# State-space steps of a small macaron network: two Vector instructions a step in place of four

## The reference, cut to what matters

```python
delta = jax.nn.softplus(jnp.einsum('blr,er->ble', dt, W_dt) + b_dt)
A = -jnp.exp(A_log)
dA = jnp.exp(delta[..., None] * A)
dBx = delta[..., None] * Bm[:, :, None, :] * xc[..., None]
def step(h, inp):
    dA_t, dBx_t = inp
    h = dA_t * h + dBx_t
    return (h, h)
y = jnp.einsum('bles,bls->ble', hs, Cm) + xc * Dp
```

## Time and profile before

| what | us |
|---|---|
| median of 3 runs | 843.04 |
| lowest, highest of them | 842.71, 849.75 |
| span of the profiled execution | 845.8 |
| VectorE busy in the span | 561.1 |
| TensorE busy in the span | 754.4 |

### The profile page before, as it was taken

The page is one execution under the profiler, slowest core; times in us unless marked ns, Lnnn a source line. Parts: engine busy times, 40 slices in busy tenths (PEclk is TensorE's granted clock), DMA queues, the critical chain, the costliest instruction groups (busy, mean ns, idle before and its releaser), DMA issues.

```text
span 845.8 us, 10714 instructions
## 1 busy us (share of the span) xinstructions
PE 754.4 (89%) x3807; PEld 522.9 (62%) x3823; DVE 561.1 (66%) x983; ACT 407.3 (48%) x600; POOL 254.9 (30%) x193
## 2 busy tenths in 40 slices
PE   4899979995789799999998999998789999788997
PEld 3587555652335366667876777775447776435775
DVE  4444699999969999975345547347854655953543
ACT  3354797666446876741232343351385432174221
POOL 0000059985436787960896000001000000000000
PEclk9899999999997999999998998999899999999999
DMA  8300022222101222216101000034000142000000
GB/s 287 109 2 1 2 63 76 73 74 66 50 27 44 66 71 70 76 50 189 43 1 21 1 1 1 13 76 111 28 2 1 52 108 66 3 27 1 1 0 26
DMA packets 30591, 41.75 MB, mean 49 GB/s; under 512 B 3753, under 2 KB 19955, under 8 KB 30515
## 3 DMA queue, kind: packets, MB, share of 16 engines
q1 hardware_dynamic: 29290, 40.91, 16.6%
q10 hardware_dynamic: 1252, 0.19, 0.2%
HBM read 36.73 MB, written 4.26 MB: 48 GB/s over the span
## 4 chain that ended last, share of the span: by engine, by line
PE 64%; DVE 14%; issue 8%; ACT 6%; DMA 5%; SPq 2%; POOL 1%; DVEq 0%; POOLq 0%; ACTq 0%
PE PS L501 34%; PE PS L868 7%; PE PS L601 3%; DVE PS L1997 3%; PE PS L1071 2%; PE PS L1054 2%; PE PS L832 2%; PE PS L646 2%; DVE shared L2005 1%; ACT shared L1580 1%; PE PS L751 1%; DMA scratch_k<-shared 1%; PE PS L852 1%; PE PS L459 1%; PE PS L936 1%
## 5 line engine op out<-in xcount | busy, mean ns | idle before, releaser
L2316 POOL TENSOR_TENSOR shared<-shared,route 128x1024 f32<-128x1024 f32 x64 | 151.4, 2370 | 78.5 <-DVE shared L2005 78.4
L501 PE MATMUL PS<-xnT,weights_r 128*128 128x256 f32 (+1 forms) x732 | 155.2, 359 | 0.5 <-issue 0.3
L501 PE MATMUL PS<-xnT,work_r 128*128 128x512 f32 (+1 forms) x596 | 153.0, 406 | 0.0
L2005 DVE TENSOR_TENSOR_SCAN shared<-shared,PS 128x512 f32<-128x512 f32 x128 | 148.8, 1204 | 0.0
L501 PEld LDWEIGHTS PS<-xnT,weights_r 128*128 128x128 f32 x732 | 114.1, 189 | 34.1 <-issue 20.6
L501 PEld LDWEIGHTS PS<-xnT,work_r 128*128 128x128 f32 (+1 forms) x596 | 112.5, 194 | 25.5 <-issue 1.3
L868 PE MATMUL PS<-shared,cf 128*128 128x512 f32 x256 | 123.3, 605 | 0.0
L1761 DVE TENSOR_TENSOR gated<-gated,PS 128x512 f32<-128x512 f32 (+1 forms) x52 | 35.7, 686 | 106.1 <-ACT gated L1239 106.1
L1239 ACT ACTIVATE gated<-PS 128x512 f32<-128x512 f32 (+1 forms) x52 | 31.1, 598 | 139.7 <-PE PS L501 132.0
L1522 ACT ACTIVATE shared<-shared,cols 128x512 f32<-128x512 f32 x128 | 83.6, 712 | 22.6 <-DVE shared L2005 18.8
L501 PE MATMUL PS<-weights_r,work_r 128*128 128x256 f32 (+1 forms) x624 | 89.5, 294 | 2.0 <-DVE work_r L1768 1.8
(11 more groups left out here) (232 smaller groups left out, 1083.2 us busy)
## 6 DMA issues: line engine op xcount, KB each, us to landing
route<-scratch_c SPq DMA_DIRECT2D x64, 256.0 KB, 3.2
shared<-in_L_ffn_W_dram SPq DMA_DIRECT2D x3, 1024.0 KB, 8.7
scratch_k<-shared SPq DMA_DIRECT2D x12, 128.0 KB
scratch_q<-shared SPq DMA_DIRECT2D x12, 128.0 KB
shared<-scratch_k SPq DMA_DIRECT2D x8, 192.0 KB
shared<-scratch_q SPq DMA_DIRECT2D x8, 192.0 KB
mamba_w<-in_L_ffn_w_dram SPq DMA_DIRECT2D x2, 704.0 KB, 5.3
beside<-in_L_ffn_w_dram SPq DMA_DIRECT2D x2, 704.0 KB, 7.7
```

Source lines behind the costliest of these rows:

```text
L501: last = nc.tensor.matmul(o, lhs[l], rhs[r], start=(start and i == 0), stop=(stop and i == 2))
L2005: v.tensor_tensor_scan(hst[:, (t % 2 * 2 + j) * T:(t % 2 * 2 + j + 1) * T], decay[t % D_SLOTS][:, j * T:(j + 1) * T], products[:, j * T:(j ...
L2316: nc.gpsimd.tensor_tensor(hc[:, u * 2 * T:(u + 1) * 2 * T].rearrange("p (c t) -> p c t", c=2), hst[:, (t % 2) * 2 * T:(t % 2 + 1) * 2 * T] ...
```

## The change

Per step VectorE issues one product with B of 1024 columns (B is read twice, by a stride of zero over the chunks) and one scan of 1024 columns. The scan runs through from the first chunk to the second. So that no state is carried across, the decay of the first token of each chunk is zero: all such columns of the ring are set to zero once, by VectorE ahead of sequence 0, and ScalarE's exponentials write only columns 1 to 511 of each chunk. The product of a step waits for the whole scan of the step before, the scan for the whole product. The semaphore counts are kept (each instruction now adds 2).

```diff
-                        nc.scalar.activation(decay[t % D_SLOTS][:, j * T:(j + 1) * T], delta_of[b][c], ACT.Exp,
+                        nc.scalar.activation(decay[t % D_SLOTS][:, j * T + 1:(j + 1) * T], delta_of[b][c][:, 1:T], ACT.Exp,
                                              scale=c_A[:, n + c * DS:n + c * DS + 1]).then_inc(s["dA"], 1)
...
+                    v.memset(decays.rearrange("p (s t) -> p s t", t=T)[:, :, 0:1], 0.0)
...
                 def times_b(t):
                     half = t // DS
                     dve.wait_ge(s["B"], base + t + 1)
-                    for j in range(2):
-                        c = 2 * half + j
-                        dve.wait_ge(s["scan"], HEAD + 2 * (base + t - 1) + j + 1)
-                        if t % DS == 0:
-                            dve.wait_ge(s[("dx", "dx_p")[half]], b * 2 + j + 1)
-                        v.tensor_tensor(products[:, j * T:(j + 1) * T], dx[:, c * T:(c + 1) * T], bank(B_BANK),
-                                        ALU.mult).then_inc(s["mul"], 1)
+                    dve.wait_ge(s["scan"], HEAD + 2 * (base + t))
+                    if t % DS == 0:
+                        dve.wait_ge(s[("dx", "dx_p")[half]], b * 2 + 2)
+                    v.tensor_tensor(products.rearrange("p (c t) -> p c t", c=2),
+                                    dx[:, 2 * half * T:(2 * half + 2) * T].rearrange("p (c t) -> p c t", c=2),
+                                    bank(B_BANK).unsqueeze(1).broadcast_to([P, 2, T]), ALU.mult).then_inc(s["mul"], 2)
 
                 def scan(t):
                     dve.wait_ge(s["hc"], HEAD + base + t - 1)
-                    for j in range(2):
-                        dve.wait_ge(s["dA"], 2 * (base + t) + j + 1)
-                        dve.wait_ge(s["mul"], HEAD + 2 * (base + t) + j + 1)
-                        v.tensor_tensor_scan(hst[:, (t % 2 * 2 + j) * T:(t % 2 * 2 + j + 1) * T],
-                                             decay[t % D_SLOTS][:, j * T:(j + 1) * T], products[:, j * T:(j + 1) * T],
-                                             0.0, ALU.mult, ALU.add).then_inc(s["scan"], 1)
+                    dve.wait_ge(s["dA"], 2 * (base + t) + 2)
+                    dve.wait_ge(s["mul"], HEAD + 2 * (base + t) + 2)
+                    v.tensor_tensor_scan(hst[:, t % 2 * 2 * T:(t % 2 + 1) * 2 * T], decay[t % D_SLOTS], products,
+                                         0.0, ALU.mult, ALU.add).then_inc(s["scan"], 2)
```

## The result

The changed kernel took 864.11 us (median of four runs, 860.7 to 864.64), the kernel before 844.96 us beside it (842.71 to 849.75). The two medians lie 19.15 us apart. The ratio worked out over the fast runs of both is 1.0196, with a 95% interval of 1.0149 to 1.0242: about 16.6 us, or 2%, slower. That the kernel is slower is clear of the noise; whether by a little less or a little more than 2% is not. A second set of runs gave 1.020 (1.014 to 1.026). The forecast was 12.4 us of loss and 855.4 us, so the direction and the kind of loss were right and the size a quarter too small. The range of 847 to 862 us was stated on a kernel before of 843.0 us: 864.11 lies 2 us above it, while 843.0 x 1.0196 = 859.6 lies inside. The profiled execution has a span of 862.9 us, 17.1 more than the 845.8 of before, and took 864.64 us in itself, 1.7 more than its span.

The account below looks back on a forecast made before the run. VectorE, full in the state-space steps, was taken as the bound; +6.5 us in sequence 0, +5.85 in sequence 1 and 0.1 for the memset made 12.4 us, so 843.0 + 12.4 = 855.4 us, range 847 to 862.

Parts of the forecast that it names:

- The bound: State-space steps: VectorE is full there and only there, and practically never waits for other engines.
- plain step: A step with no other VectorE work in between: 1.22 + 0.12 + 2.26 + 0.12 = 3.72 us for 3.42, +0.30.
- The pauses: In front of each merged product and scan on VectorE: 0.12 us each, in place of an overlap of 0.08.
- the row with the separate wait: Attention copy L2065, two waits in front, starts 0.13 us behind its neighbour; taken as the guide for 0.12.
- the row of the chain: Softplus chain: an instruction waiting for its neighbour by one semaphore starts after 0.04 us; taken as the lower bound.
- rival A: Each dependence between neighbours costs only 0.035 us: plain step 3.55 us, +3.3 us in all, 846.4 us; chance 0.14.
- the 47 steps that the sum counts: Steps 0 to 29 without other VectorE work behind: 22 in sequence 0, 25 in sequence 1, +0.30 us each.
- Steps with other work behind the scan: Eight steps in sequence 0, five in sequence 1, where the following work still overlaps: +0.10 us each.
- What came back: Shrinking VectorE waits: sequence 0, 0.46 (sums with D), 0.40 (taps); sequence 1, 0.37 (steps 3, 4), 1.06 (sums), 0.67 (end).
- Between the sequences: From step 30's product in sequence 0 the path is TensorE's, so only steps 0 to 29 count.
- Rival C: TensorE, idler in the steps, falls to 1.2 GHz in some three more stretches: +4 us, 859.4 us; chance 0.13.
- Rival B: Waits are free and fewer instructions win: a step of 3.32 us, 0.10 less, 839.5 us; chance 0.05.

Follow-up runs that it names:

- changed_again: The changed kernel as it is, run again beside the other experiments: 863.65 us against 846.73 for the kernel before, ratio 1.020.
- products_in_sbuf: The changed kernel with its products written to SBUF in place of PSUM banks 2 and 3: 934.32 us beside 847.41 for the kernel before, one run.
- zero_columns: The kernel before with only the memset of the first columns and the exponentials of 511 columns: 846.54 us beside 846.73, one run.
- count_one: The changed kernel with semaphore counts of 1 in place of 2, waits in their old order: 864.45 us beside 847.41 for the kernel before, one run.

## Why the prediction was right, and where it was short

**The bound** was read right: VectorE is full in the steps, and what a plain step gains in length comes out in the end. From the first product to the end of step 30's product in sequence 0, and from the first product to the opened banks in sequence 1, the kernel took 8.5 and 7.6 us longer, 16.1 in all, where 6.5 and 5.85 were forecast. **The pauses** were put at 0.12 each and measured 0.13. Taking the row with the separate wait over the row of the chain decided the forecast: had the chain's 0.04 been right, the loss would have been rival A's 3.3 us. The run with the neighbour's wait first has just that pause, and lost 7.6 us; so rival A's kernel exists, but it is not this one, and my sum for it was 4 us short too.

That the 0.12 came out so close is partly luck, for the earlier trace rows do not show a wait for a neighbour. The code in front of the copy L2065 (L2064 and the line before) waits for a product of TensorE and for a result of ScalarE that was long there, and the product ended at the same time as VectorE's instruction ahead:

```profile
615.50 0.86 PE L1071 MATMUL PS<-shared 128*32 128x256 f32 x16
```

It ends at 615.50 + 0.86 = 616.36, VectorE's neighbour at 616.37. The wait instruction between is one for a single semaphore (21 ns), which behind a neighbour in the steps makes 0.10; the 0.13 of the changed kernel comes from waits for two. For the product these are two only because a count of 2 leaves none in the instruction, which the prediction did not consider: with a count of 1 its pause is 0.10.

**The term that was mis-sized** is the plain step: 3.72 forecast, 3.78 measured. The scan has less fixed cost than the product, 2 x 1.204 - 2.287 = 0.12 us in place of 0.144, the product took 1.228 in place of 1.22, and both pauses are 0.01 longer. Over the 47 steps that the sum counts, 0.066 us each make 3.1. Steps with other work behind the scan grew by 0.12 to 0.15 in place of 0.10, and two of them by 0.27, some 0.7 more. One pause of 0.51 us in front of the product at 145.03, 0.38 more than elsewhere, was in no term. It comes back at the same step in both other executions with the merged pair and counts of 2 (`changed_again` and `products_in_sbuf`), so it is no chance, but its cause stays open: its wait instruction was over 0.42 us before the product started. Less some 0.4 that came back beyond the forecast (next paragraph), this makes 3.8, and the measured difference is 16.1 - 12.35 = 3.7.

**What came back** did so nearly as forecast. The waits at the sums with D and at steps 3 and 4 of sequence 1 are gone (those steps are 3.78 us like all), and at the end TensorE needed 6.86 us from the product to the banks, where 7.10 was forecast and 7.77 measured before. Ahead of the taps I had left a wait of 0.14; it went too.

**Between the sequences** I had assumed no change from the product of step 30 on. It took 25.8 us to the first product of sequence 1, for 27.2 before. Before, TensorE's fall to 1.2 GHz at 229 us lay right behind that product, on the path; after, the stretch of 232.1 to 235.5 lies ahead of the product, which ended at 237.6. The traces of the experiments bear out that the clock decides here and the change does not. In the eleven traces with this order of work the stretch from the end of step 30's product to the first product of sequence 1 has one of two lengths: 25.6 to 25.8 us where 3 to 7 us of it are at 1.2 GHz, and 27.1 to 27.5 where 10 are. `zero_columns`, with the steps of before, has 25.6, and `changed_again` 27.5.

**Rival C** gave nothing that the traces can put down to the change. From the first to the last scan of each sequence TensorE was at 1.2 GHz for 28.8 us in place of 12.4. But the kernel before with only the zero columns, whose steps are as short as before, has 23.9 us there, and the changed kernel's second trace 25.2; so executions differ in this by as much. And it cost nothing in the steps: VectorE's idle time behind TensorE's copy of B is 1.5 us, 1.4 before, as a longer step of VectorE hides a slower TensorE. Behind the steps, where VectorE is no longer full, the longer stretch at the feed-forward stage (10.3 for 6.8 us) does not explain the 2.7 us: from the opened banks to 3 us before the end, both traces have 23.9 us at 1.2 GHz in all. From the opened banks to the end the eleven traces took between 467.6 and 473.8 us, whatever their steps were like. The changed kernel's own four runs, between 860.7 and 864.64 us, show how much executions differ.

**Rival B** is out in the form in which it stood, as neighbours in the steps with a wait for each other never overlapped in any run. Its grain of truth is the 0.08 us a step that merging gives back when the waits are there anyway. The page that stood beside it, the Trainium skill's "VectorE: DVE Perf Modes", section "The DRAIN you can't avoid", says that the semaphore costs nothing extra; here the measurement decides, as two such waits a step with nothing else changed cost 21.6 us. The overlap of 0.08 without a wait, which the prediction held against the page, is no evidence against it: the same section adds that a next instruction that is not held starts earlier. The advice to cut instructions and not semaphores stands in that page's section "Rules for kernel authors".

## What to carry to other kernels

Before merging two instructions of one engine, count which waits then point at the direct neighbour: here each such wait cost 0.09 of overlap and 0.13 of pause, 0.22 us. A merge saved 0.12 to 0.14 us of fixed cost, but the overlap of 0.08 to 0.09 between its two halves went with it, so some 0.04 was left of each. For a step: 0.35 of overlaps lost and 0.27 of pauses, less 0.26 of fixed cost, is the 0.36 us by which it grew, within 0.01. If a wait for the neighbour can't be avoided, let the instruction itself carry it, by putting it first and by counting in ones; the two together took 9 of the 17 us back, and counting in ones alone (`count_one`) left 864.45 us. And read the place of inputs before moving them: PSUM for one input of a VectorE instruction was what let it run beside GpSimd.

## What the runs showed of the hardware that I had not expected

The first surprise is that how a wait is written sets the pause: 0.03, 0.10 or 0.13 us for the same dependence. The second is the scan from SBUF beside GpSimd: 4.47 us for 2.27, with GpSimd slowed as well, so that moving 1024 columns of products out of PSUM cost 934.32 - 864.45 = 70 us beside `count_one` of the same set, which takes as long as the changed kernel (one run each).
